# Two transformer-like layers over 16 batches: a new order of the stages on PE, ACT, DVE and GpSimd

## The chip, the core and the metric

The kernel runs on one core of one Trainium2 chip. The metric is the time of one execution on the device, in microseconds (us). Engines are named as the profile names them: PE is TensorE (its weight loads are PEld), DVE is VectorE, ACT is ScalarE, POOL is GpSimd, SP is SyncE, which issues only DMAs here. "The granted clock" is the share of its full speed that TensorE was granted in a stretch.

## What is computed

Sixteen batches of 548 tokens (36 of an image, 512 of text, 64 numbers each) pass through two layers. Each line adds its result to `h`:

```
h = concat(patches @ W + b, table[x_txt] + positions)
h = h + attention(layernorm(h))          # relu attention, FFN 64->128->64, layernorm
h = h + experts_top1(layernorm(h))       # argmax expert of 8, 1370 slots each, relu MLP 64->256->64
h = h + linear_attention(layernorm(h))   # per-head k and v normalised, kv = k^T v, q kv, proj, gelu
h = h + experts_top2(layernorm(h))       # 8 experts of 64->256->64 with gelu, weights of the best two
```

Only the second expert layer is computed densely: all eight experts see every token, and the two chosen ones are weighted. The first one moves tokens: each token's normalised row is scattered to its expert's slots in DRAM, the slots are computed, and each token gathers its row back.

## The kernel before, in words

The work is written as small stages, one function each, for a batch or a unit. `t1`, `q`, `k`, `scores0` to `scores4`, `attend_a` to `attend_c`, `ffn1`, `gate`, `count` are PE's in layer one; `norm1a`, `q_low`, `resid`, `norm3a`, `place` are DVE's there. `place` finds each token's slot; POOL's `scatter_a` and `scatter_b` then write the rows, five indirect DMAs a batch (L1079). Between the layers stands stage B: 32 units of the first expert layer, each turned (`b_turn`, L1322), multiplied (`b_up`, L1140 and L1141), multiplied back (`b_down`, L1340) and turned back (`b_back`, L1347). POOL gathers the rows of each batch (L497).

Layer two runs, for each batch: `mixed` on DVE (L430 to L442, L758 and L760: the gathered rows are weighted, limited and added to `H`), `mixed_stats`, `norm4` (L778 to L781), `t4` and `kv` on PE (L1111, L1118), `kv_b` (L788), `square` on ACT (L683), `sum_squares` (L794), `roots_kv` (ACT L664), `kvnorm_inv` and `kvnorm` (L799 to L808), `gram` (PE L563), `gram_s` (L816), small products, `pre_bias` (L847), `gelu_proj` (ACT L689), `norm5`, `t5`, `route` (L602) with its DVE stages, and then the dense experts: 18 tiles of 8 units, each unit `up` (PE L1140 and L1141), `gelu` (ACT L715), `down` (PE L628, two units at a time), `weigh` (DVE L978), `summed` (POOL L538); `back` and `finish` (DVE L990) close a tile. The dense experts of one batch run beside the linear attention of later ones.

Some stages stand once: `moe_bias` on PE (L1307), `moe_gains` (L1586, L1589) and `low_moe` (L1595) on DVE, `high_w` (L1466) and `high_moe` (L1470) on ACT prepare the weights of the experts. `fill` is three matmuls of ones (L1147) whose result nobody reads; 44 of them stand at numbered places.

What sets the order on each engine is a table, not the code. Each stage has a time in a period of 32 (for batch b, 32 b is added), each (stage, number) may have an entry in `..._MOVED` that is added to it, and `in_order` sorts:

```
plan.append((when + b * PERIOD + moved.get((name, b), 0), len(plan), name, b))
...
return [(name, b) for _, _, name, b in sorted(plan)]
```

Each engine runs its list strictly in order; its stages wait on semaphores that count the stages of other engines. A bank of PSUM is taken by `banks.take`, which makes the stage wait for the reader of the stage that took the bank before it in this order. ACT has three sets of functions in use (Sqrt, Gelu, Exp; Identity and Relu are in all), and where its list goes from a function of one set to one of another, an ACT_TABLE_LOAD stands in between.

Of the kernel before, what the change touches and what calls it, by code (L numbers as in the profile page):

```python
# [60 lines left out]
           mixed=12, weighted=5, norm4=3, kvnorm=3, fold=3, resid2=11, norm5=4, route_a=11, route_b=6)  # L61
# [73 lines left out]
def early_fusion_kernel(nc, i, out):  # L135
    with ExitStack() as ctx:
# [106 lines left out]
        def at(s):  # L243
# [11 lines left out]
        POOL_ONE = ((8.25, "gather_a"), (18.5, "gather_b"), (134.75, "offset"), (384, "scatter_a"), (396.75, "scatter_b"))  # L255
        PE_ONE = ((93.75, "t1"), (106.5, "q"), (115, "k"), (130, "scores0"), (132.5, "v"), (136, "scores1"), (140.25, "scores2"),
                  (145.25, "attend_a"), (150.75, "scores3"), (153.5, "attend_b"), (155.5, "scores4"), (162.5, "attend_c"), (170.25, "o_turn"),
                  (185.25, "t2"), (189.5, "ffn1"), (203.5, "ffn2"), (217, "y_turn"), (273, "t3"), (273.25, "gate"), (286.5, "count"))
        ACT_ONE = ((47.25, "roots1"), (98.5, "stack1"), (108.25, "q_high"), (123, "k_high"), (137, "relu0"), (139, "relu1"), (144.5, "relu2"),
                   (154.25, "relu3"), (159.5, "relu4"), (168, "o_copy"), (189.25, "stack2"), (198.5, "ffn_relu"), (207, "y_copy"), (226.5, "root2"),  # L260
                   (253.75, "root3"), (275.5, "stack3"))
        DVE_ONE = ((25.25, "norm1a"), (41.75, "norm1b"), (104, "q_low"), (112.25, "k_low"), (127.25, "vals"), (168.75, "resid"), (212.25, "norm2a"),
                   (226.25, "norm2b"), (237.25, "norm3a"), (254.75, "norm3b"), (268.5, "gate"), (285.75, "place"))
# [114 lines left out]
        gram_s, kv_g, kv_s, a_s, fold_b = ff[0][0:D + 1, 0:D + 1], ff[0][0:D, 128:128 + D], ff[0][0:D, 256:256 + D], ff[0][0:D, 384:384 + D + 1], ff[1][:, 0:D]  # L378
# [1493 lines left out]
```

## Time and profile before

| | |
|---|---|
| median of 3 runs | 848.64 us (847.61 to 850.04) |
| span of the profiled execution, first to last instruction | 846.4 us |
| PE busy | 729.7 us, 86% of the span |
| DVE busy | 612.2 us, 72% |
| ACT busy | 481.7 us, 57% |
| POOL busy | 433.1 us, 51% |
| mean granted clock of TensorE | 0.935 |

The profiled execution has no other time of its own than its span. The median of the runs is 2.2 us above it, which is what lies around the first and last instruction; a time that is worked out within the span is to be read with these 2.2 us added. In the run of time, layer one takes 0 to 287 us, stage B 298 to 372 us, the start of layer two 372 to 474 us, and from there the tiles of the dense experts end every 25 us or so until the last two (images) close the span.

### The profile page before, as it was taken

Reading aid. Unit: us, or ns where it says so; the run is one execution under the profiler, and the core shown is the slowest. Engines: PE = TensorE matmul, PEld = TensorE weight load, DVE = VectorE, ACT = ScalarE, POOL = GpSimd, SP = SyncE. Lnnn points to the kernel's source line nnn. Section 1 sums busy time; section 2 is a strip of 40 time slices with the busy share of each in tenths; the row PEclk is TensorE's granted clock in tenths of the full one; section 3 lists DMA queues with packets and bytes.
Section 4 is the critical chain, followed back from the end, with each engine's and each line's share of the span. In section 5 each row is a group of like instructions: output and inputs, shape, how many; then the busy total and the mean of one; then the engine's idle time right before and its main releaser. Section 6 shows DMA issues by size and latency. Waiting matters only on the chain.

```text
span 846.4 us, 15831 instructions
## 1 busy us (share of the span) xinstructions
PE 729.7 (86%) x4619; PEld 487.1 (58%) x4619; DVE 612.2 (72%) x2308; ACT 481.7 (57%) x980; POOL 433.1 (51%) x470
## 2 busy tenths in 40 slices
PE   3589999999988689965789989989989999899995
PEld 1366777666655257643456555556555656566672
DVE  4557899989678536576777889888888977786231
ACT  1255655555541146642246877766788666777552
POOL 5732617773764600246646667667676763223222
PEclk8599999999997889995679999999999999999988
DMA  7910000000000023220022221222221122223200
GB/s 216 359 53 9 14 8 19 22 21 5 5 4 3 4 58 97 75 66 12 6 57 57 62 56 17 57 59 63 62 63 41 31 55 61 62 62 61 62 14 7
DMA packets 60976, 43.69 MB, mean 52 GB/s; under 512 B 29100, under 2 KB 56252, under 8 KB 60636
## 3 DMA queue, kind: packets, MB, share of 16 engines
q1 hardware_dynamic: 51820, 36.35, 17.2%
q0 software_dynamic: 7200, 4.17, 2.4%
q10 hardware_dynamic: 1872, 2.18, 0.9%
q8 instruction: 38, 0.62, 0.3%
q14 instruction: 46, 0.38, 0.1%
HBM read 31.66 MB, written 13.47 MB: 53 GB/s over the span
## 4 chain that ended last, share of the span: by engine, by line
PE 26%; ACT 15%; DVE 14%; issue 9%; POOL 2%; DMA 1%; DVEq 0%; ACTq 0%; POOLq 0%
ACT scratch L715 7%; PE psum L628 6%; PE psum L1140 5%; PE psum L1141 4%; ACT L715 3%; PE psum L1340 3%; ACT L664 2%; PE psum L1147 2%; DVE xt L788 1%; PE psum L1322 1%; PE psum L1118 1%; PE psum L602 1%; ACT L659 1%; DVE kh L885 1%; DVE stats L1507 1%
## 5 line engine op out<-in xcount | busy, mean ns | idle before, releaser
L715 ACT ACTIVATE scratch<-psum,fb 128x512 f32<-128x512 f32 (+2 forms) x288 | 172.2, 665 | 37.4 <-PE psum L1141 36.1
L628 PE MATMUL psum<-scratch,w_fw 128*64 128x256 f32 (+2 forms) x1152 | 141.7, 383 | 11.4 <-DVE scratch L978 5.7
L538 POOL TENSOR_TENSOR prob<-prob,scratch 128x256 f32<-128x256 f32 (+2 forms) x126 | 79.3, 629 | 141.0 <-DVE scratch L978 139.4
L497 POOL DMA_INDIRECT uu<-expert_out,slot_i x80 | 83.2, 1040 | 88.3 <-issue 68.7
L1079 POOL DMA_INDIRECT slots_buf<-xt,slot_i x80 | 82.5, 1032 | 68.0 <-DVE slot_i L1754 45.8
L628 PEld LDWEIGHTS psum<-scratch,w_fw 128*64 128x64 f32 x1152 | 79.1, 140 | 56.5 <-DVE scratch L978 13.5
L1065 POOL DMA_INDIRECT emb<-in_table,w_ids x64 | 63.4, 991 | 55.8 <-DVE stats L1507 33.5
L1405 ACT ACTIVATE prob<-psum 128x292 f32<-128x292 f32 (+1 forms) x160 | 55.1, 396 | 52.2 <-PE psum L1207 52.1
L1140 PE MATMUL psum<-kh,fw_hi 128*128 128x512 f32 x176 | 80.0, 455 | 0.6 <-ACT scratch L715 0.5
L1141 PE MATMUL psum<-kh,fw_lo 128*128 128x512 f32 x176 | 71.8, 408 | 0.0
L978 DVE SCALAR_TENSOR_TENSOR scratch<-psum,w_fb,X 128x256 f32<-128x256 f32 (+1 forms) x119 | 54.4, 460 | 16.9 <-PE psum L628 15.5
L1206 PE MATMUL psum<-qst,kh 128*128 128x292 f32 (+1 forms) x160 | 53.8, 350 | 2.4 <-DVE kl L1635 1.2
L1216 PE MATMUL psum<-prob,vv 128*64 128x256 f32 (+1 forms) x320 | 49.8, 410 | 1.3 <-ACT prob L1405 1.3
L683 ACT ACTIVATE xt<-xt 128x640 f32<-128x640 f32 x16 | 11.8, 737 | 63.8 <-DVE xt L788 63.8
L1507 DVE BATCH_NORM_STATS2 stats<-H 128x6 f32<-128x64 f32 x320 | 46.6, 213 | 1.5 <-issue 0.4
L1140 PEld LDWEIGHTS psum<-kh,fw_hi 128*128 128x128 f32 x176 | 34.5, 196 | 19.3 <-ACT scratch L715 6.8
L1140 PE MATMUL psum<-kl,fw_hi 128*128 128x512 f32 (+2 forms) x112 | 45.4, 411 | 0.0
L1766 DVE TENSOR_TENSOR qst<-psum,qst 64x256 fp32r<-64x256 f32 (+2 forms) x32 | 16.5, 518 | 37.8 <-ACT qst L1490 37.7
L1207 PE MATMUL psum<-qst,kl 128*128 128x292 f32 (+1 forms) x160 | 43.4, 292 | 0.0
L1147 PE MATMUL psum<-ones_b 128*128 128x512 bf16 x132 | 38.8, 436 | 3.3 <-ACT scratch L715 2.0
L1141 PE MATMUL psum<-kl,fw_lo 128*128 128x512 f32 (+2 forms) x112 | 41.5, 378 | 0.0
L1206 PEld LDWEIGHTS psum<-qst,kh 128*128 128x128 f32 x160 | 30.7, 192 | 17.9 <-issue 12.9
(272 smaller groups left out, 1715.7 us busy)
## 6 DMA issues: line engine op xcount, KB each, us to landing
X<-share_buf SPq DMA_DIRECT2D x32, 512.0 KB
slots_buf<-zeros SPq DMA_DIRECT2D x8, 352.0 KB, 4.9
expert_out<-zeros SPq DMA_DIRECT2D x8, 352.0 KB, 4.9
out<-H SPq DMA_DIRECT2D x16, 128.0 KB
X<-in_patches ACTq DMA_DIRECT2D x3, 576.0 KB, 7.3
slots_buf<-xt,slot_i POOLq DMA_INDIRECT x80, 2.2
uu<-expert_out,slot_i POOLq DMA_INDIRECT x80, 2.5
emb<-in_table,w_ids POOLq DMA_INDIRECT x64
```

The costliest lines, as they stand in the source:

```text
L497: pool.indirect_dma_start(yg[b % 2][0:rows, s, :], None, expert_out, bass.IndirectOffsetOnAxis(slot_i[0:rows, b, (s + 1) % SLOTS:(s + 1) % ...
L538: pool.tensor_tensor(total[t % 2][:, 0:z], total[t % 2][:, 0:z], part[m % PARTS][:, 0:z], ALU.add).then_inc(sem("summed"), 1)
L628: last = pe.matmul(bank(6 + n % 2)[h * D:(h + 1) * D, 0:z], w["fw2"][:, e * J + j, :], hid[(J * n + j) % (J * UNITS)][:, h * z:(h + 1) * z ...
L715: act.activation(hid[m % (J * UNITS)][:, 0:z], bank(2 + m % 4)[:, 0:z], ACT.Gelu, bias=fb1[:, e * J + j:e * J + j + 1]).then_inc(sem("gelu ...
L1065: pool.indirect_dma_start(emb[b % 2][:, t, :], None, i["table"], bass.IndirectOffsetOnAxis(w["ids"][:, b * TXT + t:b * TXT + t + 1], 0)).t ...
L1079: pool.indirect_dma_start(slots_buf, bass.IndirectOffsetOnAxis(slot_i[0:rows, b, (s + 1) % SLOTS:(s + 1) % SLOTS + 1], 0), xt3[b % XT3][0: ...
L1140: pe.matmul(dst, parts[0][:, cols], rhs, start=True, stop=False)
L1141: return pe.matmul(dst, parts[1][:, cols], rhs, start=False, stop=True)
L1147: pe.matmul(bank(FILLED).rearrange("p (k n) -> p k n", k=4), ones_b[:], bs(ones_b[:], 4), start=True, stop=True)
L1206: pe.matmul(dst, kh[b % 2][:, at(s):at(s) + P], q_side, start=True, stop=False)
L1405: act.activation(prob[s][:, FIRST[h]:FIRST[h] + z], bank(SCORE[h])[:, 0:z], ACT.Relu, scale=SCALE).then_inc(sem("relu"), 1)
L1507: st(dve.bn_stats(stats[:, s, :], src[:, s, :]))
```

## The change: what it does

The tables POOL_ONE, PE_ONE, ACT_ONE, DVE_ONE (layer one), POOL_TWO, PE_TWO, ACT_TWO, DVE_TWO (layer two) and the four MOVED tables have other numbers; the MOVED tables grow from some 50 lines to some 400, with an entry for nearly every stage and batch. Nothing else in the file changes: the functions, the once-tables, the lists of fills and the lags of the experts' units are as they were. Line numbers of the new file are those of the old one plus 348 behind the tables (L1147 is now L1495, L1589 is L1937, L788 is L1136, L715 is L1063).

```diff
-        PE_ONE = ((93.75, "t1"), (106.5, "q"), (115, "k"), (130, "scores0"), (132.5, "v"), (136, "scores1"), (140.25, "scores2"),
+        PE_ONE = ((80.125, "t1"), (107.25, "q"), (119.125, "k"), (136.875, "scores0"), (119.875, "v"), (141.375, "scores1"), (145.75, "scores2"),
...
-        PE_TWO = ((74.25, "t4"), (78.75, "kv"), (94, "gram"), (97.5, "gains_k"), (101.5, "by_q"), (104.75, "by_proj"), (114.5, "proj"), (130, "t5"),
+        PE_TWO = ((74.125, "t4"), (83, "kv"), (101.375, "gram"), (105, "gains_k"), (108.5, "by_q"), (111.875, "by_proj"), (120.375, "proj"),
```

Of the MOVED tables, new entries are for instance `("moe_bias", 0): -599.839` on PE, `("moe_gains", 0): -559.402` and `("low_moe", 0): -571.34` on DVE, `("high_moe", 0): -659.064` on ACT: these stages go from the end of layer one to its start. `("fill", 16): -3.257` to `("fill", 35): -189.54` gather fills ahead of stage B, and `("up", 0): -26.809` brings the first unit of the dense experts forward.

Every engine has the same stages as before. The only instructions whose number differs are ACT's table loads: 60 before, 72 now.

**Place one, the end of layer one.** DVE before, at the last but one batch: statistics of `norm3a`, then `moe_gains` (L1586, L1589), then the gate (L1719 on).

```order
L1674 TENSOR_TENSOR zt<-zt,rs 128x320
L1676 TENSOR_TENSOR zt<-zt,w_fg 128x320
L1679 TENSOR_TENSOR H<-H,zt 128x320
L1507 BN_STATS stats<-H 128x6 x5
L1510 BN_AGGR mv_1<-stats 128x2 x5
L1586 TENSOR_TENSOR fb1<-psum,w_fb1 128x16
L1589 TENSOR_SCALAR scratch<-scratch,w_fln_g 128x256 x8
L1591 ISA
L1719 TENSOR_TENSOR g_lg<-psum,w_gb 128x40
```

DVE now, at the same place:

```order
L2022 TENSOR_TENSOR zt<-zt,rs 128x320
L2024 TENSOR_TENSOR zt<-zt,w_fg 128x320
L2027 TENSOR_TENSOR H<-H,zt 128x320
L1855 BN_STATS stats<-H 128x6 x5
L1858 BN_AGGR mv_1<-stats 128x2 x5
L2067 TENSOR_TENSOR g_lg<-psum,w_gb 128x40
L2069 TENSOR_REDUCE g_mx<-g_lg 128x5
```

`moe_gains` now stands behind `norm1a` of batch 4, near the start; `low_moe` (L1595), which stood between the last gate and the last `place`, stands behind `k_low` of batch 2.

PE before, from the last `count` (L1297, L1300) to the first `b_turn` (L1322) of stage B:

```order
L1147 MATMUL psum<-ones_b 128x512 x3
L1297 MATMUL psum<-oh_b,tri_b 128x40
...
L1300 MATMUL psum<-oh_b,ones_b 128x8
L1147 MATMUL psum<-ones_b 128x512 x30
L1322 MATMUL psum<-w_ident,X 64x128 x6
L1140 MATMUL psum<-qst,ew_hi 128x384
L1141 MATMUL psum<-qst,ew_lo 128x384
```

PE now, at the same place:

```order
L1495 MATMUL psum<-ones_b 128x512 x3
L1645 MATMUL psum<-oh_b,tri_b 128x40
...
L1648 MATMUL psum<-oh_b,ones_b 128x8
L1495 MATMUL psum<-ones_b 128x512 x69
L1670 MATMUL psum<-w_ident,X 64x128 x6
L1495 MATMUL psum<-ones_b 128x512 x3
L1488 MATMUL psum<-qst,ew_hi 128x384
L1489 MATMUL psum<-qst,ew_lo 128x384
```

There are 69 matmuls of ones ahead of the first `b_turn` where 30 stood, and no fills further on in stage B.

**Place two, the start of layer two.** PE before, from the last `b_back` (L1347): `t4` (L1111) and `kv` (L1118) of batch 0, then `gram` (L563) of batch 0, and `t4` of batch 1 only behind the small products.

```order
L1347 MATMUL psum<-w_ident,X 128x128 x2
L1147 MATMUL psum<-ones_b 128x512 x3
L1111 MATMUL psum<-w_ident,xt 128x128 x3
L1118 MATMUL psum<-w_wkv,ot 128x256 x2
L1118 MATMUL psum<-w_wkv,ot 36x128
L1147 MATMUL psum<-ones_b 128x512 x3
L563 MATMUL psum<-scratch 65x65 x5
L569 MATMUL psum<-ff,ak 64x65
```

PE now:

```order
L1459 MATMUL psum<-w_ident,xt 128x128 x3
L1695 MATMUL psum<-w_ident,X 128x128
L1495 MATMUL psum<-ones_b 128x512 x3
L1466 MATMUL psum<-w_wkv,ot 128x256 x2
L1466 MATMUL psum<-w_wkv,ot 36x128
L1495 MATMUL psum<-ones_b 128x512 x21
L1459 MATMUL psum<-w_ident,xt 128x128 x3
L1466 MATMUL psum<-w_wkv,ot 128x256 x2
L1466 MATMUL psum<-w_wkv,ot 36x128
L911 MATMUL psum<-scratch 65x65 x5
```

`t4` of batch 0 now stands ahead of the last `b_back`, and `t4` and `kv` of batch 1 ahead of `gram` of batch 0. The first `up` (L1140, now L1488) stood behind `route` and the small products of batches 1 and 2; now it stands right behind `route` of batch 0 (L950, L951). On DVE the same place reads, before (`norm4`, `mixed`, statistics, `kv_b`, `sum_squares`):

```order
L781 TENSOR_TENSOR xt<-zt,rs 128x320
L430 TENSOR_TENSOR uu<-uu,top_w 128x320
...
L760 TENSOR_TENSOR H<-H,prob 128x320
L1507 BN_STATS stats<-H 128x6 x5
L1510 BN_AGGR mv_1<-stats 128x2 x5
L788 TENSOR_TENSOR xt<-psum,w_kv_b 128x640
L794 TENSOR_REDUCE prob<-xt 128x160
L799 TENSOR_SCALAR prob<-prob 128x160
```

and now:

```order
L2130 COPY X<-psum 128x128 x2
L1136 TENSOR_TENSOR xt<-psum,w_kv_b 128x640
L778 TENSOR_TENSOR uu<-uu,top_w 128x320
...
L1108 TENSOR_TENSOR H<-H,prob 128x320
L1855 BN_STATS stats<-H 128x6 x5
L1858 BN_AGGR mv_1<-stats 128x2 x5
L1142 TENSOR_REDUCE prob<-xt 128x160
L1126 RECIPROCAL rs<-sd_1 128x5
L1127 TENSOR_TENSOR zt<-H,mv_1 128x320
```

`kv_b` of batch 0 (L788, now L1136) stood behind `mixed` of batch 1 and stands ahead of it; `norm4` of batch 1 (now L1126) stands right behind the statistics it needs.

**Place three, ACT in the tiles of the dense experts.** Before, one batch's worth: the loads go to Sqrt for `roots_kv` (L664), to Gelu (L715), to Sqrt for `roots4` (L659), to Gelu.

```order
L715 ACTIVATE scratch<-psum,fb 128x512 x2
L664 ACT_TABLE_LOAD
L664 ACTIVATE prob<-prob 128x160
L670 ACTIVATE sd_0<-mv_0,eps_t 128x5
L671 ACTIVATE sd_0<-mv_0,eps_t 128x5
L715 ACT_TABLE_LOAD
L715 ACTIVATE scratch<-psum,fb 128x512 x4
L725 ACTIVATE ff<-psum 40x128
L659 ACT_TABLE_LOAD
L659 ACTIVATE sd_0<-mv_0,eps_t 128x5
L715 ACT_TABLE_LOAD
L715 ACTIVATE scratch<-psum,fb 128x512 x2
```

Now, in one of the early tiles, `roots5` (L1018, L1019) no longer stands beside `roots_kv` (L1012), and has loads of its own:

```order
L1012 ACT_TABLE_LOAD
L1012 ACTIVATE prob<-prob 128x160
L1063 ACT_TABLE_LOAD
L1063 ACTIVATE scratch<-psum,fb 128x512 x2
L1037 ACTIVATE vv<-vv 128x320
L1063 ACTIVATE scratch<-psum,fb 128x512 x4
L1018 ACT_TABLE_LOAD
L1018 ACTIVATE sd_1<-mv_1,eps_t 128x5
L1019 ACTIVATE sd_1<-mv_1,eps_t 128x5
L1073 ACTIVATE ff<-psum 40x128
L1063 ACT_TABLE_LOAD
L1063 ACTIVATE scratch<-psum,fb 128x512 x2
```

Six loads stand in a batch's worth instead of four, in about six of the tiles; two fewer stand in a few late ones; the sum is the 12 more.

## Rows read from the trace of the kernel before

**Rows 1.** The page's head and part 1.
```profile
span 846.4 us, 15831 instructions
PE 729.7 (86%) x4619; PEld 487.1 (58%) x4619; DVE 612.2 (72%) x2308; ACT 481.7 (57%) x980; POOL 433.1 (51%) x470
```
**Rows 2.** Stretches: from:to, length, each engine's busy us (instructions), clock, DMA share, GB/s.
```profile
0.00:42.00 42.00, 19.35 (x86) 12.08 (x86) 20.38 (x102) 9.50 (x21) 26.98 (x32) 0.72 0.88 287
42.00:85.00 43.00, 39.15 (x241) 27.57 (x242) 29.70 (x117) 23.78 (x66) 14.60 (x16) 1.00 0.11 34
296.00:339.00 43.00, 39.84 (x291) 28.30 (x292) 20.46 (x58) 25.33 (x55) 0.00 (x0) 0.92 0.27 77
```
**Rows 3.** The same view, for layer two: its start, two periods, its end.
```profile
372.00:434.00 62.00, 36.78 (x156) 20.93 (x155) 44.94 (x161) 13.93 (x29) 35.73 (x35) 0.66 0.14 30
434.00:472.00 38.00, 34.65 (x207) 23.25 (x208) 29.55 (x121) 28.08 (x48) 22.58 (x25) 0.96 0.16 33
472.00:497.00 25.00, 22.52 (x146) 14.62 (x146) 21.49 (x77) 18.43 (x32) 17.53 (x20) 1.00 0.25 54
797.00:822.00 25.00, 25.00 (x198) 18.78 (x195) 7.17 (x18) 13.53 (x33) 6.18 (x14) 0.87 0.26 55
```
**Rows 4.** Timeline of DVE, end of layer one: start us, us, operation, idle before.
```profile
264.33 0.20 DVE L1719 TENSOR_TENSOR g_lg<-psum,w_gb 128x40 f32<-128x40 f32 x1 [1.27 <-PE psum L1130]
...
274.58 2.60 DVE L1589 TENSOR_SCALAR scratch<-scratch,w_fln_g 128x256 f32<-128x256 f32 x8
...
283.29 2.28 DVE L1595 TENSOR_TENSOR fw_lo<-scratch,fw_hi 128x2048 fp32r<-128x2048 f32 x1
```
**Rows 5.** Timeline of ACT and of POOL, end of layer one.
```profile
280.86 1.90 ACT L1470 ACTIVATE fw_hi<-scratch 128x2048 fp32r<-128x2048 f32 x1
...
281.94 0.99 POOL L1079 DMA_INDIRECT slots_buf<-xt,slot_i  x1 [3.92 <-DVE slot_i L1754]
...
294.34 0.91 POOL L1079 DMA_INDIRECT slots_buf<-xt,slot_i  x1 [0.30 <-issue]
```
**Rows 6.** Timeline of PE, end of layer one and start of stage B.
```profile
266.59 4.37 PE L1307 MATMUL psum<-w_fln_b,scratch 64*128 64x1 f32 x32
...
283.68 8.04 PE L1147 MATMUL psum<-ones_b 128*128 128x512 bf16 x30
298.51 1.46 PE L1322 MATMUL psum<-w_ident,X 128*64 128x128 f32 x6 [6.79 <-issue]
...
305.23 1.08 PE L1340 MATMUL psum<-scratch,w_ew 128*64 128x256 f32 x8
```
**Rows 7.** Timeline of DVE, start of layer two.
```profile
374.86 0.49 DVE L430 TENSOR_TENSOR uu<-uu,top_w 128x320 f32<-128x320 f32 x1 [1.68 <-DMA uu<-expert_out,slot_i]
...
379.08 0.79 DVE L788 TENSOR_TENSOR xt<-psum,w_kv_b 128x640 f32<-128x640 f32 x1
...
387.62 0.19 DVE L778 RECIPROCAL rs<-sd 128x5 f32<-128x5 f32 x1 [0.25 <-issue]
```
**Rows 8.** Timeline of PE, start of layer two.
```profile
384.42 1.52 PE L563 MATMUL psum<-scratch 128*65 128x65 f32 x10 [7.78 <-DVE scratch L808]
...
433.63 0.79 PE L1140 MATMUL psum<-kh,fw_hi 128*128 128x512 f32 x1
```
**Rows 9.** Timeline of DVE: `finish` of the first tile and of the second.
```profile
473.94 0.41 DVE L990 TENSOR_TENSOR H<-H,psum 128x256 f32<-128x256 f32 x1
...
498.81 0.41 DVE L990 TENSOR_TENSOR H<-H,psum 128x256 f32<-128x256 f32 x1
```
**Rows 10.** ACT by lines: the costliest group of table loads (busy, mean ns, idle before).
```profile
L715 ACT ACT_TABLE_LOAD x27 | 34.6, 1283 | 0.5
```
**Rows 11.** Timeline of ACT in a period of layer two.
```profile
568.02 1.27 ACT L715 ACTIVATE scratch<-psum,fb 128x512 f32<-128x512 f32 x2
569.31 1.28 ACT L664 ACT_TABLE_LOAD   x1
570.60 0.34 ACT L664 ACTIVATE prob<-prob 128x160 f32<-128x160 f32 x1
```

More of the change, by code:

```diff
@@ L259, in early_fusion_kernel @@
[L259 to L263, printed above, removed]
+        POOL_ONE = ((-45.875, "gather_a"), (-38.875, "gather_b"), (81.375, "offset"), (317.5, "scatter_a"), (345.375, "scatter_b"))
@@ L283, in early_fusion_kernel @@
-        PE_MOVED = {("attend_b", 0): -1.5, ("attend_b", 14): 2, ("attend_c", 0): -2, ("attend_c", 15): 1.5, ("back", 16): 1, ("back", 17): 14,
-                    ("by_q", 0): 3, ("by_q", 1): 0.75, ("by_q", 2): -0.25, ("by_q", 3): 0.75, ("count", 1): -3, ("count", 12): 1, ("down", 130): 4,
-                    ("down", 131): 4, ("down", 132): 3, ("down", 133): 3, ("down", 134): 3, ("down", 135): 3, ("down", 136): 8, ("down", 137): 8,
-                    ("down", 138): 8, ("down", 139): 8, ("down", 141): 8, ("down", 143): 8, ("ffn1", 1): -0.75, ("ffn1", 15): 3, ("ffn2", 13): -1.5,
-                    ("ffn2", 15): -1.25, ("gains_k", 0): 4.25, ("gains_k", 1): -0.5, ("gains_k", 15): 0.5, ("gains_k", 2): -0.75, ("gate", 15): -6,
-                    ("gram", 0): -8.5, ("gram", 1): 0.5, ("gram", 2): -0.75, ("gram", 3): 2.75, ("kv", 1): -2, ("kv", 3): 0.75, ("o_turn", 1): 5,
-                    ("o_turn", 14): -0.5, ("o_turn", 15): -2.5, ("o_turn", 2): 6, ("proj", 2): 0.75, ("proj", 3): 1.25, ("route", 1): -2.5,
[5 rows of a table removed]
@@ new lines, in early_fusion_kernel @@
+        DVE_TWO = ((33.558, "mixed"), (43.225, "mixed_stats"), (49.125, "norm4"), (85.375, "kv_b"), (90.375, "sum_squares"), (95.625, "kvnorm_inv"),
+                   (98.75, "kvnorm"), (103.75, "gram_s"), (106.25, "own_heads"), (109.75, "add_input"), (113.5, "fold"), (124.08, "pre_bias"),
+                   (126.375, "resid2"), (127.25, "resid2_stats"), (135.125, "norm5"), (140.5, "low5_even"), (141.125, "low5_odd"),
+                   (144.25, "route_logits"), (147.375, "route_first"), (151.25, "route_next"), (156.125, "route_second"), (159.125, "route_shares"))
```

345 lines of the change are left out of this document (301 added, 44 removed), and 130 rows, old and new, of tables (ACT_MOVED, DVE_MOVED, PE_MOVED).

## Prediction, made before the changed kernel ran

> **What bounds the kernel now.** I read the shares of the engines first, then the stretches, then the places where an engine stood idle. PE is busy 86% of the span, DVE 72%, ACT 57% and POOL 51% [rows 1], but these are averages over stages with different limits. In layer one PE hardly stops: 39.15 of 43 us from 42 us on at full clock [rows 2], so an order that only shuffles stages there has little to give. Only its first 42 us are loose: PE 19.35, DVE 20.38, ACT 9.50 us busy, with the DMA engines at 0.88 [rows 2]. Stage B is PE's too (39.84 of 43 us [rows 2], most of the rest before its first matmuls). Two places are not bound by any engine's work. At the start of stage B, PE ends its fills near 291.7 (283.68 and 8.04 us) and stands 6.79 us until the slots' rows come at 298.51 [rows 6]. In the start of layer two, 372 to 434 us, PE is busy 36.78 of 62 us, fills among it, and DVE 44.94, at a granted clock of 0.66 [rows 3]: there the chain of small stages of the first batches sets the pace, and the dense experts, which could fill PE, begin only at 433.63 [rows 8]. Then the tiles come at a period of 24.87 us (from 473.94 to 498.81 [rows 9]); per 25 us PE is busy 22.52, DVE 21.49, ACT 18.43 [rows 3]. No engine is full: the wait goes round between them. At the end PE is full again, 25.00 of 25 [rows 3].
>
> **The change part by part.**
>
> *The stages that stand once.* `moe_bias` (4.37 us of PE [rows 6]), `moe_gains` and `low_moe` (2.60 and 2.28 us of DVE [rows 4]) and `high_moe` (1.90 us of ACT [rows 5]) go from the end of layer one to its start. There they fall on engines that are less than half busy, so I cost them at nothing. If that cover is gone, because the weights land late under the 0.88 of DMA, PE stands in front of `moe_bias` and all batches shift; the bounds for this are 0 and 4.4 us, nearer 0. At the other end, DVE's row up to the last slots becomes shorter by 2.60 + 2.28 = 4.9 us, and the 1.27 us idle before the gate [rows 4] can be filled as well. But the slots are not the only thing the last scatters wait for. POOL issues ten scatters from 281.94 to 294.34 + 0.91 [rows 5], 1.28 us each, and needs these 13.3 us from the moment the first slots of batch 14 exist. Those come earlier by the 2.60 us of `moe_gains` and part of the 1.27, so the last scatter ends 2.8 to 3.5 us earlier. The rows of the first unit then lie ready near 295 to 295.7, in place of 298.5.
>
> *The fills ahead of stage B.* 69 matmuls stand where 30 stood. The 30 took 8.04 us [rows 6], 0.268 each; 69 take 18.5 us at that rate. The last `count`, right behind which the fills began at 283.68, follows the gate and comes 4.9 us earlier with it, near 278.7, so PE is free at 297.2 by this rate; the rate itself may be better if the clock is (I allow 2 us). So the fills reach about as far as the data, 295 to 297. This gains 1.4 to 3.5 us at the first `b_turn`, and because PE has not stood idle before, the first units do not run at the lower clock as they do before; with two fills no longer standing ahead of `b_down`, which begins at 305.23 only [rows 6], that is another 1 to 2.5 us. I take 3.5 us for this place together; bounds 0 (fills longer than the data) and 6.
>
> *Stage B itself.* The order of `b_turn`, `b_up`, `b_down`, `b_back` was a regular round of four and is irregular now (two `b_turn` in a row, two `b_back` in a row). PE was full there, so it can only lose: I take 1.5 us, bounds 0 and 3.
>
> *The start of layer two.* Before, `kv_b` of batch 0 at 379.08 stood behind `mixed` and the statistics of batch 1, which themselves waited 1.68 us for a gather from 374.86 [rows 7]. Now it stands ahead, and can run as soon as PE gives it: `t4` of batch 0 lies inside stage B now, and behind the last `b_back` (372) only a fill and `kv` are left, so near 373.6. The 4.2 us of `mixed` and statistics come behind it, so `sum_squares` of batch 0, and with it `gram` (384.42, after 7.78 us of idle PE [rows 8]), gains only about 1 us. The gain is in batch 1: its `norm4`, at 387.62 before [rows 7], follows its statistics at once, near 381; its `kv` is on PE before `gram` of batch 0. Batch 2 follows the same way, by my count of the stages between some 10 us earlier. The first `up`, at 433.63 [rows 8], stands right behind `route` of batch 0 and can begin near 407. That does not shorten the span by 26 us: in 372 to 472 us DVE has 44.94 + 29.55 = 74.5 us of work [rows 3], and what is left idle, 25 us in 100, is all that can be won. The expert units of tile 0 are now fed between the small stages. Summing DVE's stages in the new order up to the first `finish`, with the durations of before, gives about 461 in place of 473.94 [rows 9], but with 3.6 us of DVE's work for later batches not yet done. I take a lead of 10 us, bounds 5 and 14.
>
> *The steady periods.* PE's order hardly changes there; DVE's `mixed` and `norm4` come earlier, and the units are grouped unevenly. What costs is on ACT: 12 more table loads, nearly all in tiles of the first half. A load takes 1.283 us [rows 10], and nothing beside it: the ACTIVATE before ends at 569.29, the load begins at 569.31, the next ACTIVATE at 570.60 [rows 11]. Together 12 x 1.283 = 15.4 us of ACT. A tile with six loads has ACT at 18.43 + 2.6 = 21.0 of 24.9 us, still less than PE or DVE, so most of it is hidden. But `gelu` feeds `down` and `weigh`, and a load in front of it is a delay in the round that sets the period. I take a sixth of it less what the earlier `norm4` gives back: 2 us lost; bounds -12 (PE's idle 2.4 us a period, over 13 periods, won back by nearly half) and +12 (most loads on the path).
>
> The Trainium skill, "ScalarE: Activation LUTs", section "What ACT_TABLE_LOAD costs", counts a drain of about 1380 ns with each load of about 1283 ns, 2.66 us for a switch. The load agrees with the trace, the drain does not show in it, since the next instruction begins where the load ends; by the page's figure the 12 loads would be an estimated 32 us of ACT, and the forecast sum would turn into a loss if half of that were on the path. I go by the rows.
>
> *The end* is full of PE's work in nearly the same order, so a lead that is there at 797 us is kept.
>
> The sum: -3.5 +1.5 -10 +2 = -10 us, against the profiled span of 846.4: 836.4, and with the 2.2 us that the median lies above that span, 838.6 us.
>
> **The rivals.**
>
> *ACT's loads eat the lead (slower).* If each extra load falls into the round (the `gelu` of a unit waits, PE's `down` waits for it, DVE's `weigh` for that), 15.4 us [rows 10] are lost, more than the 12 won elsewhere: -3.5 +1.5 -10 +15.4 = +3.4, 852.0 us. The point from which it decides is a tile whose ACT has more than the period of 24.87 us in work and waits for `xt`; for it speaks that a load stands between two ACTIVATEs with no slack on either side [rows 11], against it ACT's 6.6 idle us of 25 [rows 3].
>
> *An uneven layer one loses (slower).* PE is busy 39.15 of 43 us there [rows 2] and each engine runs strictly in order, so a stage placed ahead of its data stops its engine. With 1 us for each of 13 batches, 848.6 - 10 + 13 = 851.6. For it speaks that single entries move a stage by whole periods; against it that stages of one batch lie many microseconds apart, with other batches between them.
>
> *The periods shrink too (faster).* If the new order takes half of PE's 2.4 idle us of each of 13 periods, 15.6 us more and no 2 us lost: 838.6 - 17.6 = 821.0. For it: neither PE nor DVE is full. Against: PE's own order is nearly the old one, and ACT has more to do.
>
> *The lead is given back (no change).* The early `up` units run ahead, and then wait in the first periods for `share` rows, DMAs on SP's queue, or a bank; finish of tile 5 comes where it did. Then only stage B's part is left, and 848.6 - 2 = 846.6 or more, up to 850.
>
> **How the numbers follow.** My forecast has 0.50, its own range 829 to 848. The loads 0.18, layer one 0.10, shrinking periods 0.12, the lead given back 0.10. A difference of less than 0.3%, 2.5 us, can't be told from no change. Faster: nearly all of the forecast (0.47), all of the shrinking periods (0.12) and a little of the others (0.04), 0.63. Slower: most of the two slower rivals, 0.25. The same: 0.12. The range reaches from 825 (half of the fast rival is left out) to 853 (a third of the slow ones is left out).
>
> **What would show it.** In the changed kernel's profile: the last scatter ends near 292; the first `b_turn` begins at 295 to 297, with less than 2 us idle before it and a clock near full; `kv_b` of batch 0 within 3 us of the last `b_back`; the first `up` near 407; the first `finish` near 458 (461 less the 3 us won before), so 15 or 16 us before its old place, a part of which is not real; and the sixth `finish` about 12 us before its old place. It is wrong if stage B begins later than 298.5, if PE's busy share in 42 to 254 us falls by more than 2 points, or if the period of tiles 1 to 4 is over 25.5 us; then the loads have got into the round.

## The result: 30 us less, three times what was forecast

The new order takes 819.15 us (median of 4 runs, 817.05 to 823.86) against 849.34 us of the kernel before (847.61 to 851.33): a ratio of 0.965, with a 95% interval of 0.9616 to 0.9685. Run again later, beside other kernels, it took 816.75 us, a ratio of 0.9621 (0.9592 to 0.9651). The forecast was 838.6 us with a range of 825 to 853; the measured time lies below it, next to the number of the rival that had the periods shrink (821.0 us, chance 0.12), which it meets in part by luck, as is worked out below.

The page of the new kernel, its head and part 1, against [rows 1]:

```profile
span 822.1 us, 15850 instructions
PE 731.4 (89%) x4619; PEld 500.8 (61%) x4619; DVE 631.0 (77%) x2308; ACT 499.2 (61%) x992; POOL 435.9 (53%) x470
```

The matmuls are the same 4619, PE's busy time is 1.7 us more, and the span is 24.3 us less: the change took away PE's idle time, 116.7 us before and 90.7 now. This profiled execution, with its span of 822.1 us, is the longest of its four runs. A second profile of the same kernel, from the later runs, has a span of 813.3 us and is the shortest of its six. Both begin stage B at the same time to 0.04 us, and they part in stage B and layer two (the first has a stretch of lower clock, 0.80 against 0.93 for 522 to 547 us), by up to 8.8 us at the end. So a number that comes from layer two is good here to about 4 us to either side, and where only one profile is used, the text says which.

The end of layer one and the start of stage B in the first profile of the new kernel, timeline of POOL and of PE, against [rows 5, 6]:

```profile
285.88 0.92 POOL L1427 DMA_INDIRECT slots_buf<-xt,slot_i  x1 [0.30 <-issue]
```
```profile
277.38 15.98 PE L1495 MATMUL psum<-ones_b 128*128 128x512 bf16 x69
293.20 0.82 PE L1670 MATMUL psum<-w_ident,X 128*64 128x128 f32 x6
...
297.29 1.08 PE L1688 MATMUL psum<-scratch,w_ew 128*64 128x256 f32 x8
```

The last scatter ends at 286.80 in place of 295.25: 8.5 us earlier, where I had forecast 2.8 to 3.5. The first `b_turn` follows at 293.20 and the first `b_down` at 297.29, 7.9 us earlier. The single stages stand at the start now (timelines of PE and of DVE; L1655 is `moe_bias`, L1483 the `k` behind it, L1943 `low_moe`), against [rows 4, 6]. `high_w` on ACT moves as well, from 91.67 to 36.15 us, which my prediction did not list:

```profile
26.35 6.98 PE L1655 MATMUL psum<-w_fln_b,scratch 64*128 64x1 f32 x32
33.27 2.20 PE L1483 MATMUL psum<-xs,w_wk 128*128 128x292 f32 x4
```
```profile
58.40 2.28 DVE L1943 TENSOR_TENSOR fw_lo<-scratch,fw_hi 128x2048 fp32r<-128x2048 f32 x1
```

The start of layer two in the first profile, timelines of DVE and of PE, against [rows 7, 8]. L1136 is `kv_b` of batch 0, L1126 `norm4` of batch 1, L911 `gram` of batch 0, L1488 the first `up`:

```profile
368.19 0.82 DVE L1136 TENSOR_TENSOR xt<-psum,w_kv_b 128x640 f32<-128x640 f32 x1 [1.60 <-PE psum L1466]
...
373.84 0.18 DVE L1126 RECIPROCAL rs<-sd 128x5 f32<-128x5 f32 x1
```
```profile
380.06 1.55 PE L911 MATMUL psum<-scratch 128*65 128x65 f32 x10 [0.92 <-DVE xt L1136]
...
400.32 0.79 PE L1488 MATMUL psum<-kh,fw_hi 128*128 128x512 f32 x1
```

Stretches of both kernels between the same events, the later profile of the new kernel below (its columns are those of [rows 2]). The events are the first `b_turn`, the last copy of stage B, `finish` of tile 0 and of tile 8, and the end (the two `finish` to 0.6 us):

```profile
42.00:298.50 256.50, 230.34 (x1484) 160.69 (x1485) 204.30 (x854) 127.62 (x341) 139.19 (x135) 0.97 0.06 15
298.50:371.90 73.40, 71.58 (x533) 49.67 (x534) 42.01 (x120) 46.51 (x98) 9.67 (x10) 0.97 0.27 78
371.90:473.90 102.00, 73.43 (x374) 45.40 (x372) 76.46 (x283) 43.90 (x79) 60.04 (x60) 0.78 0.15 31
473.90:672.90 199.00, 180.56 (x1136) 116.92 (x1135) 171.03 (x608) 145.70 (x249) 138.96 (x152) 0.99 0.25 53
672.90:846.40 173.50, 154.46 (x1011) 102.32 (x1009) 98.00 (x344) 108.48 (x195) 58.20 (x83) 0.95 0.23 48
```
```profile
0.00:42.00 42.00, 26.31 (x124) 20.42 (x125) 23.28 (x118) 11.54 (x25) 24.61 (x29) 0.76 0.89 286
42.00:293.20 251.20, 229.49 (x1478) 164.02 (x1477) 210.32 (x838) 127.45 (x337) 138.92 (x138) 0.97 0.07 16
293.20:364.90 71.70, 70.16 (x529) 48.28 (x528) 44.33 (x124) 44.97 (x99) 10.90 (x11) 1.00 0.27 78
364.90:451.30 86.40, 67.57 (x336) 43.16 (x336) 72.52 (x260) 45.18 (x77) 60.36 (x60) 0.76 0.16 35
451.30:647.30 196.00, 180.96 (x1154) 119.40 (x1149) 179.75 (x641) 156.94 (x258) 154.28 (x164) 0.99 0.25 54
647.30:813.30 166.00, 150.37 (x1009) 102.13 (x1007) 98.36 (x331) 112.92 (x199) 45.50 (x70) 0.95 0.23 50
```

Length less PE's busy time is PE's idle time. Before and now: 22.6 and 15.7 in the first 42 us, 26.2 and 21.7 in the rest of layer one, 1.8 and 1.5 in stage B, 28.6 and 18.8 in the start of layer two, 18.4 and 15.0 in tiles 1 to 8, 19.0 and 15.6 behind them. Idle time fell in every part of the program but stage B, where the first profile has 2.9. I had seen a part of the first and the fourth, and had put down the tiles as a small loss.

These numbers count the matmuls of ones, which nobody reads, as work. They take PE 21.3 us before and 27.6 now (later profile) in layer one, 3.3 and 1.3 in stage B, and 14.2 and 5.3 in the start of layer two. So more than half of the 11.4 us that went from PE's idle time in layer one was filled with them, and idle time and fills together fell there by 5.2 us only. In the start of layer two they fell by 18.7, while 3 us more of real work stand in a stretch that is 15.6 us shorter.

The lead of `finish`, the time by which it comes earlier (`finish` of 474, 499, 648, 673, 700 and 837 us of before; the first and the fourth row below answer to [rows 9]):

| | tile 0 | tile 1 | tile 7 | tile 8 | tile 9 | tile 15 |
|---|---|---|---|---|---|---|
| new kernel, first profile | 19.1 | 13.9 | 13.9 | 18.3 | 25.4 | 24.3 |
| new kernel, later profile | 22.5 | 17.3 | 21.1 | 25.6 | 32.6 | 33.1 |

As forecast, tile 0's lead is partly not real, and 5 us of it are gone at tile 1. Then the first profile has no net change up to tile 7 and the later one 3.8 us more, and in both 11.5 us are won in tiles 8 and 9.

### The profile page after: what moved, and what is told of

It is laid out like the page before. It is cut to its first block and busy times, and to the rows that moved or that the text cites. A ratio compares the mean times of both kernels' runs of the same rounds, so it can differ in the third digit from the quotient of the medians.

```text
span 822.1 us, 15850 instructions
## 1 busy us (share of the span) xinstructions
PE 731.4 (89%) x4619; PEld 500.8 (61%) x4619; DVE 631.0 (77%) x2308; ACT 499.2 (61%) x992; POOL 435.9 (53%) x470
## 5 line engine op out<-in xcount | busy, mean ns | idle before, releaser
L1063 ACT ACTIVATE scratch<-psum,fb 128x512 f32<-128x512 f32 (+2 forms) x288 | 172.9, 667 | 54.5 <-PE psum L1489 45.8
L976 PE MATMUL psum<-scratch,w_fw 128*64 128x256 f32 (+2 forms) x1152 | 144.9, 393 | 5.9 <-DVE prob L1326 4.1
L886 POOL TENSOR_TENSOR prob<-prob,scratch 128x256 f32<-128x256 f32 (+2 forms) x126 | 82.2, 652 | 107.8 <-DVE scratch L1326 102.3
L1427 POOL DMA_INDIRECT slots_buf<-xt,slot_i x80 | 80.4, 1004 | 67.1 <-DVE slot_i L2102 45.5
L976 PEld LDWEIGHTS psum<-scratch,w_fw 128*64 128x64 f32 x1152 | 83.6, 144 | 47.8 <-issue 16.3
L1488 PE MATMUL psum<-kh,fw_hi 128*128 128x512 f32 x176 | 80.2, 456 | 1.9 <-ACT scratch L1063 1.9
L1326 DVE SCALAR_TENSOR_TENSOR scratch<-psum,w_fb,X 128x256 f32<-128x256 f32 (+1 forms) x119 | 53.6, 464 | 25.6 <-PE psum L976 24.8
L1753 ACT ACTIVATE prob<-psum 128x292 f32<-128x292 f32 (+1 forms) x160 | 55.0, 398 | 25.8 <-PE psum L1555 24.4
L1488 PE MATMUL psum<-kl,fw_hi 128*128 128x512 f32 (+2 forms) x112 | 47.5, 428 | 1.5 <-ACT scratch L1063 1.5
L1564 PE MATMUL psum<-prob,vv 128*64 128x256 f32 (+1 forms) x320 | 47.4, 405 | 0.0
L1847 ACT ACTIVATE scratch<-psum,w_eb 128x256 f32<-128x256 f32 (+2 forms) x64 | 32.0, 550 | 24.7 <-PE psum L1489 24.3
L1488 PEld LDWEIGHTS psum<-kh,fw_hi 128*128 128x128 f32 x176 | 34.7, 197 | 18.5 <-ACT scratch L1063 6.9
L1063 ACT ACT_TABLE_LOAD x32 | 41.1, 1283 | 4.5 <-PE psum L976 4.0
L1489 PE MATMUL psum<-kl,fw_lo 128*128 128x512 f32 (+2 forms) x112 | 43.2, 389 | 0.0
L875 POOL TENSOR_TENSOR ex<-euler,mx 128x5 f32<-128x5 f32 x16 | 19.4, 1212 | 38.6 <-DVE lg L1281 38.2
L1554 PEld LDWEIGHTS psum<-qst,kh 128*128 128x128 f32 x160 | 30.7, 192 | 12.2 <-issue 5.5
```

Source lines behind the costliest of these rows:

```text
L886: pool.tensor_tensor(total[t % 2][:, 0:z], total[t % 2][:, 0:z], part[m % PARTS][:, 0:z], ALU.add).then_inc(sem("summed"), 1)
L976: last = pe.matmul(bank(6 + n % 2)[h * D:(h + 1) * D, 0:z], w["fw2"][:, e * J + j, :], hid[(J * n + j) % (J * UNITS)][:, h * z:(h + 1) * z ...
L1063: act.activation(hid[m % (J * UNITS)][:, 0:z], bank(2 + m % 4)[:, 0:z], ACT.Gelu, bias=fb1[:, e * J + j:e * J + j + 1]).then_inc(sem("gelu ...
L1326: dve.scalar_tensor_tensor(out=dst[:, 0:z], in0=bank(6 + n % 2)[:, 0:z], scalar=w["fb2"][:, e:e + 1], in1=tile_share(t, e)[:, 0:z], op0=AL ...
L1427: pool.indirect_dma_start(slots_buf, bass.IndirectOffsetOnAxis(slot_i[0:rows, b, (s + 1) % SLOTS:(s + 1) % SLOTS + 1], 0), xt3[b % XT3][0: ...
L1488: pe.matmul(dst, parts[0][:, cols], rhs, start=True, stop=False)
```

## The experiments

In the first six, whole pieces of the order were taken from one kernel or the other. The old tables stand beside the new ones, and on each engine layer two follows one order for its first stages (the number in CUT) and the other for the rest:

```diff
+def in_order(engine, layer, new, old, others=()):
+    if layer == "ONE":
+        return by_times(*(new if ONE_IS == "new" else old), others)
+    first, rest = (by_times(*(new if which == "new" else old), others) for which in (FIRST_IS, REST_IS))
+    ahead = first[:CUT[engine]]
+    return ahead + [stage for stage in rest if stage not in ahead]
```

All ratios are to the kernel before in the same job.

**Layer one new, the rest old** (`ONE_IS = 'new'; FIRST_IS, REST_IS = 'old', 'old'`).

> Layer one in the new order, stage B and layer two in the old one. Theory A (the gain is a sum over places): the lead that the new kernel has when its first b_down begins, 7.9 us (297.29 against 305.23), is made by layer one and by the fills ahead of stage B; only the first is here, so slot_i of the last batches comes near 279 in place of 287, stage B begins 5 to 8 us earlier and all of it is kept: the kernel before less 5 to 8 us. Rival B (the lead is made by the fills alone, layer one is worth what the moved single stages are worth): less 3 us or nothing.

838.82 us against 849.54, a ratio of 0.987 (0.984 to 0.9899): 10.7 us less. The lead is 10.3 us at the last slots, 8.6 through stage B and 7.2 to the end. Theory A holds, and layer one is worth more than either theory gave it. This kernel has 39 matmuls of ones ahead of the first `b_turn`, nine more than before, but they end while the rows are still on their way: PE stands 5.36 us behind them, and `b_turn` begins 3.3 us after the last scatter, as before. So its lead owes nothing to the fills.

**Layer one old, the rest new** (`'old'; 'new', 'new'`).

> Layer one in the old order, stage B and layer two in the new one. Theory A: what is left of the 24 to 30 us when layer one's 6 to 8 us are taken off, so the kernel before less 17 to 22 us. Rival B: less 22 to 27 us. If the two parts do not add up (e1 and e2 together more than 4 us from the whole), the places are not independent.

827.03 us, 0.9738 (0.9713 to 0.9763): 22.5 us less. The two parts together give 33.2, the whole 30.2: they add up within what is measured. A part of the 3.0 us can be named: here 60 matmuls of ones end just as the rows come, and the time from the last scatter to the first `b_down` is 7.4 us, where it is 10.0 before and 10.5 in the new kernel, whose 69 run beyond the data.

**Stage B and the start of layer two new** (`'old'; 'new', 'old'`, CUT PE 231, DVE 215, ACT 125, POOL 60).

> Layer one old; stage B and the first stages of layer two, up to about the first finish, in the new order; all that comes later in the old order. Theory A: the lead of finish of tile 1 and later (14 us in the new kernel, 5 to 6 of them from layer one) is made here and kept to the end, so less 8 to 11 us. Rival C (a lead made early is given back unless the later order uses it): less 0 to 4 us.

837.52 us, 0.9856 (0.9829 to 0.9884): 12.0 us less. `finish` of tile 1 leads by 9.3, of tile 8 by 9.1 and of tile 15 by 10.0: a lead is kept, and is not given back. Timeline of PE in this kernel, the fills and the first `b_turn`:

```profile
282.97 14.47 PE L1584 MATMUL psum<-ones_b 128*128 128x512 bf16 x60
297.75 1.01 PE L1759 MATMUL psum<-w_ident,X 128*64 128x128 f32 x6 [0.31 <-issue]
```

From the last scatter (294.52) to the first `b_down` (301.83) it takes 7.3 us in place of 10.0. The first `b_down` leads by 3.4 us, the last copy of stage B (370.54) by 1.4, and the rest is won in the start of layer two. My forecast had 8.5 us for stage B and the start of layer two (-10 +1.5). That part was right.

**Only the end of layer two new** (`'old'; 'old', 'new'`, CUT PE 351, DVE 381, ACT 214, POOL 141).

> Layer one, stage B and layer two up to about its middle (batch 10, tile 6) in the old order, the rest in the new one. Theory A: tiles 9 to 11 of the new kernel take 12 us less than before, the last ones give 6 back, so less 6 to 12 us. Rival C (the late order gains only because it comes with a lead and with the stages that stand ahead of it): within 3 us of the kernel before, or slower.

855.69 us, 1.0075 (1.0048 to 1.0102): 6.2 us more. But the trace shows two things: `finish` of tile 7 is 20.2 us late, and that of tile 11 only 2.9. The seam, where stages of batches 11 and 12 that the new order wants later and the old one had not done meet, costs 17 us (between 620 and 670 us ACT waits 7.3 us in one piece for a batch's statistics, and PE 7.5 us for a `gelu`), and the new order wins them back in four tiles. In the last four it loses 6.8 us again, as the new kernel does in its first profile (31.1 us of lead at tile 11, 24.3 at tile 15), so some of what tiles 8 to 11 win is work put off. Neither theory had the seam.

**New up to about tile 7** (CUT PE 369, DVE 407, ACT 228, POOL 158).

> Layer one old; stage B and layer two in the new order until about tile 7's middle, the rest old. With the new order up to the first finish only, the kernel took 12.0 us less than before; with all of layer two new 22.5 less. If the late tiles (8 to 11, 25 us each before, 20 to 21 in the new order) make the difference: 12 to 14 less than before. If the middle tiles have already prepared it (stages of later batches done ahead): 18 to 22 less.

834.27 us against 850.86, 0.9802 (0.9753 to 0.9851): 16.6 us less, between the two expectations, with an interval that meets that of the start alone. In the trace, `finish` of tile 8 leads by 8.3 and of tile 15 by 10.5, no more than with the start alone, but the profiled run is the slowest of the four (837.79 us). So whether the tiles up to 7 give nothing or some 4 us stays open.

**New up to about tile 9** (CUT PE 440, DVE 497, ACT 279, POOL 191).

> Layer one old; layer two new until about finish of tile 9, the rest old. With the new order to the first finish 12.0 us less than before, to tile 7 16.6 less, throughout 22.5 less. If the gain is made in tiles 8 and 9 (periods of about 20 us in the new order against 25 before): 19 to 23 less. If only the last tiles (10 to 17) make it: 12 to 17 less.

827.69 us against 849.74, 0.9741 (0.9702 to 0.978): 22.0 us less, all that the new layer two gives. Its `finish` leads by 14.7 at tile 7, 19.2 at tile 8, 26.2 at tile 9, and then by 19 to the end. The 10 us that come on top of the start are made in the tiles up to 9. The 11.5 us of tiles 8 and 9 come alike in all four profiles that have the new order there, but here 7 of them go again in tiles 10 and 11, where the old order sets in. The share of the tiles up to 7 can't be told from profiles: with the same order up to there, `finish` of tile 7 leads by 6.5, 7.4 and 14.7 us in three kernels. The last tiles add nothing.

**Single stages moved alone, in the kernel before.**

```diff
+        PE_MOVED = {("moe_bias", 0): -580.5, ...
+        DVE_MOVED = {("moe_gains", 0): -587.75, ("low_moe", 0): -586.2, ...
+        ACT_MOVED = {("high_w", 0): -145.1, ("high_moe", 0): -663, ...
```

> The kernel before with only the single stages moved from the end of layer one to its start: moe_bias, moe_gains, low_moe, high_w, high_moe. My prediction priced this at 2.8 to 3.5 us at the last scatter, against nothing at the start; stage B then begins about 3 us earlier: less 2.5 to 3.5 us. Rival: PE or DVE wait for the weights at the start (the DMA engines are busy 0.88 there) and the batches shift: less 0 to 1 us, or slower.

859.12 us against 849.39, 1.0116 (1.0052 to 1.018): 9.7 us more. Here `moe_bias` stands behind `v` of batch 0. Timelines of DVE and ACT in this kernel:

```profile
45.47 0.17 DVE L1586 TENSOR_TENSOR fb<-psum,w_fb 128x16 f32<-128x16 f32 x1 [6.42 <-PE psum L1307]
```
```profile
46.26 0.81 ACT L1405 ACTIVATE prob<-psum 128x292 f32<-128x292 f32 x2 [8.49 <-PE psum L1207]
```

DVE stood 6.42 us for `moe_bias`, and ACT 8.49 us for the scores behind it. `k` of the seventh batch and of all later ones comes 14.6 to 14.8 us later. At the end of layer one 4.7 us of that are won back (10.1 us at the last slots), near the 4.9 that I had counted, and 3.6 at the last scatter (306.41 for 295.25), for which I had 2.8 to 3.5. So the end of the move was priced right, and the start, which I had at nothing, was wrong for this place.

**The same with `moe_bias` ahead of `k` of batch 0** (`("moe_bias", 0): -598.6`), in the place where PE stood idle 4.97 us.

> The kernel before with the single stages moved to the start, but moe_bias ahead of k of batch 0, where PE stood idle 4.97 us, in place of behind v of batch 0. If what cost 14.8 us at the start in the first try was mostly PE's 4.4 us falling behind work: the batches shift by 7 to 11 us, and the kernel takes 2 to 6 us more than before. If DVE's and ACT's parts (moe_gains, low_moe, high_w, high_moe ahead of q_low and k_low) cost it: as in the first try, 8 to 10 us more.

852.99 us against 849.74, 1.0039 (1.0018 to 1.006): 3.3 us more. Timeline of PE in this kernel:

```profile
26.82 6.99 PE L1307 MATMUL psum<-w_fln_b,scratch 64*128 64x1 f32 x32
```

In the gap it takes 6.99 us, in place of 4.37 at the end of layer one [rows 6], and costs 2.3 us at `vals` of batch 0. The later batches shift by 9.0 us. The rest of the price, some 6 us, I put down to the stages on DVE and ACT; no run moves them alone. At the last slots 3.0 us are left. So even in its gap the move does not pay in the old layer one. In the new one it stands at the same place (26.35, until 33.27), and the last slots come earlier all the same.

**39 more matmuls of ones**, with the single stages moved as in the first try (`FILLS_B = (*[-23.5] * 13, ...)`).

> The same and 39 more matmuls of ones ahead of the first b_turn (69 in all, as in the new kernel). If the clock and not the data holds the first units of stage B: 1.5 to 3 us less than the kernel with the single stages moved alone, with the first b_down near 299 to 301. Rival: the fills last longer than the rows take to come, and it is the same or slower than without them.

856.68 us, 1.0082 (1.0054 to 1.011): 2.4 us less than without them, which their intervals do not tell apart. The traces give a cleaner measure, the time from the end of the last scatter to the first `b_down`: 10.0 us before (295.25 to 305.23), 10.0 with the single stages moved (306.41 to 316.43), 9.1 with the fills (304.53 to 313.67), and 10.5 in the new kernel (286.80 to 297.29).

**Fewer fills in the new kernel**, 54 matmuls in place of 69.

```diff
+        LEFT_OUT = range(20, 25)
-            return [(when, "fill", first + k) for k, when in enumerate(sorted(times))]
+            return [(when, "fill", first + k) for k, when in enumerate(sorted(times)) if first + k not in LEFT_OUT]
```

> The new kernel with 54 matmuls of ones ahead of the first b_turn in place of 69 (five fills left out). In the new kernel the last scatter ends at 286.8 and PE is busy with fills until 293.2, while before the rows came 3.3 us behind the last scatter. So the data is there near 290, and stage B begins 3 us earlier: 3 us less than the new kernel. Rival: the rows come only near 293 and nothing changes.

814.43 us, 0.9583 (0.9521 to 0.9644). Timeline of PE:

```profile
277.40 12.44 PE L1496 MATMUL psum<-ones_b 128*128 128x512 bf16 x54
289.88 0.49 PE L1671 MATMUL psum<-w_ident,X 128*64 128x128 f32 x3
...
290.68 0.52 PE L1671 MATMUL psum<-w_ident,X 128*64 128x128 f32 x3 [0.31 <-DMA X<-slots_buf]
...
293.96 1.08 PE L1689 MATMUL psum<-scratch,w_ew 128*64 128x256 f32 x8
```

PE leaves the fills as the rows arrive: it waits 0.31 us for the second of them. The time from the last scatter to the first `b_down` is 7.3 us (286.66 to 293.96), 3.2 less than in the new kernel. The fills of the new kernel were too long by just these. What 69 of them gave against 30 was nothing with this layer one; 60 gave 2.6 us with the old one, where the rows come later. Both kernels were run again on one chip.

> The new kernel once more, beside the one with fewer fills on the same chip: 0.960 to 0.970 of the kernel before.

> The new kernel with 54 in place of 69 matmuls of ones ahead of stage B, again, beside the new kernel itself: 3 to 5 us less than it, since the first b_turn began 3.3 us earlier (289.88 against 293.20) and the lead was kept to the end. If it is less than 1 us, the first run's 4.7 us were the measurement's.

816.75 us, 0.9621 (0.9592 to 0.9651), for the new kernel and 814.5 us, 0.9581 (0.9551 to 0.9611), with fewer fills: 2.3 us less, where the first traces give 3.3 at the first `b_turn` and the second pair 4.6 (288.62 against 293.24, of which 1.4 are an earlier last scatter). The intervals overlap, but both are ratios to the same runs of before. Six runs against six, the means are 817.2 and 814.2 us, 2.9 apart, with a 95% interval of some 0.7 to 5.2: that it beats the new kernel is shown, by how much is not. In the second trace the 54 fills end 1.2 us before the rows come. It beats the kernel before by 35 us.

**Twelve more table loads in the kernel before, by a moved stage.**

```diff
+        ACT_MOVED = {**{("roots5", b): 4 for b in range(4, 10)}, ...
```

> The kernel before with roots5 of batches 4 to 9 moved behind one more pair of units, so that it needs table loads of its own: 12 more loads, 72 in all, as the new kernel has. If all of them were on the path: 15.4 us more. My prediction took about a sixth of it, 2 to 3 us more. If the period is held by something else and a load is hidden: within 1.5 us of the kernel before.

862.28 us, 1.0182 (1.0105 to 1.026): 12.9 us more. `finish` goes from 1.6 us early at tile 1 to 15.0 late at tile 10, 16.6 us for 12 loads. What PE waits for in this kernel (525 to 663 us: us in total, times, longest), and the same row of before (524 to 648 us):

```profile
PE psum L569 <- DVE ff L816: 11.4, 5, 2.4
```
```profile
PE psum L569 <- DVE ff L816: 2.0, 5, 0.4
```

The wait is for `gram_s`, which stands behind `norm5` on DVE, and that waits 8.9 us in five times for the moved `roots5`, where no such wait shows before. So this run does not tell a load's price from that of a late stage.

**Twelve more loads and nothing moved**, in the kernel before and in the new one.

```diff
             def gelu(n):
+                if n in (13, 21, 29, 35, 43, 53):
+                    act.activation(roots_spare[:, n // POS:n // POS + 1], eps_t[:, 0:1], ACT.Sqrt)
```

> The kernel before with a Sqrt of one column, which nobody reads, ahead of six units' gelu (units 13, 21, 29, 35, 43, 53): 12 more loads and 6 tiny ACTIVATEs, no stage moved. If the load itself was the price in the run with roots5 moved (16.6 us): 15 to 17 us more. If that price came from roots5 being late, with DVE's norm5 and gram_s waiting behind it: 0 to 6 us more.

> The new kernel with the same six Sqrts ahead of the same units: 84 loads. If the new order hides a load: 0 to 4 us more than the new kernel, and less than what the same edit costs the old order. If loads are on the path in both: 12 to 17 us more.

Old order: 867.58 us against 850.86, 1.0224 (1.0171 to 1.0277), 16.7 us more, or 1.39 a load. New order: 829.2 us, 0.9767 (0.972 to 0.9813), which is 0.0117 above the new kernel's first ratio and 0.0146 above its later one, so 10 to 12 us, or 0.8 to 1.0 a load. Both prices are good to 4 or 5 us. I had let five sixths of a load be hidden. In the old order nearly nothing of it is. That the new order hides up to a third is likely and not shown. What PE waits for with the added loads in 455 to 700 us, in the new order, and in the same stretch of the new kernel's first profile:

```profile
PE psum L1490 <- ACT scratch L1063: 15.1, 9, 3.1
```
```profile
PE psum L1488 <- ACT scratch L1063: 3.4, 6, 1.3
```

`up` waits for `gelu` to free its bank, 11.7 us more.

**Eight loads fewer in the new kernel**, by `roots4` of four batches moved beside other stages of its set.

```diff
+        ACT_MOVED.update({('roots4', 4): -2.353, ('roots4', 5): 1.978, ('roots4', 6): -9.24, ('roots4', 8): -5.069})
```

> The new kernel with four of ACT's stages moved beside another that uses the same set: roots4 of batch 4 behind roots5 of batch 1, of 5 behind roots_kv of 4, of 6 behind roots5 of 3, of 8 behind roots5 of 5. 64 table loads in place of 72. If a load costs 1.38 us here as it did in the old order (16.6 us for 12): 11 us less than the new kernel. If ACT waits for PE anyway in these tiles (it waits 16.6 us for up there), or the moved roots4 now waits for its statistics or delays what stands behind it: no gain, or up to 8 us slower.

840.73 us, 0.9907 (0.9874 to 0.9939): some 21 us more than the new kernel by the ratios, with fewer loads. `finish` of tile 0 is 3.2 us late against the first profile, tile 1 12.0, tile 4 14.6, and it stays there: all is lost where the first stages moved stand. Timeline of ACT, `roots4` of batch 6, and what ACT waited for in 400 to 520 us, here and in the new kernel:

```profile
470.60 0.30 ACT L1008 ACTIVATE sd<-mv,eps_t 128x5 f32<-128x5 f32 x1 [6.37 <-DVE mv L1859]
```
```profile
ACT sd L1008 <- DVE mv L1859: 15.8, 3, 6.4
```
```profile
ACT sd L1007 <- DVE mv L1858: 4.3, 1, 4.3
```

Moved ahead of its statistics, it stops ACT for 6.37 us with the `gelu` of all units behind it, more than the two loads (2.6 us) that it saves.

## Why the prediction was wrong, and where it was right

*The single stages and the end of layer one.* The step that failed first is "I cost them at nothing", with the scatters 2.8 to 3.5 us earlier. In the old layer one the start costs 9.0 to 14.8 us at the middle batches and 3.3 to 9.7 us in all. Engines busy for less than half of 42 us are not cover: what counts is which stage is next behind the inserted one. The end gave about the 4.9 us counted (4.7 and 6.0 measured at the last slots). But the new layer one as a whole has its last slots 7.7 to 10.7 us earlier, in the seven profiles of kernels that share it. So its other moves must absorb the start's price and win 3 to 6 us beyond the 4.9; I had them at 0. PE's idle time in layer one fell by 11.4 us (22.6 + 26.2 to 15.7 + 21.7), against 6 us more of busy time, and the fills alone are 6.2 us more. Which of the moved stages does it, no run here tells.

*The fills.* I forecast PE in the fills to 295 to 297 with the data at 295; PE left them at 293.20. The rate was better than I took, 15.98 us for 69, but the data was there near 290. The step was mis-sized because it rested on the last scatter. The term in sum, -3.5 us, measured -7.9 at the first `b_down`, and its split was wrong: -8.5 from layer one and +0.5 from the fills. The reasoning behind the fills' own part holds where they end with the data: with 60 of them and the old layer one the way from the last scatter to the first `b_down` shrank by 2.6 us, and the first six `b_turn` matmuls took 1.01 us in place of 1.46. Not two fills but one left the way to `b_down`: one still stands at 293.86.

*Stage B.* Taken at 1.5 us lost. In the first profile the lead falls from 7.9 to 5.6 (371.91 against 366.30), 2.3 us; in the later one from 7.9 to 7.1. In the third run it falls from 3.4 to 1.4. Right, as far as it can be told.

*The start of layer two.* Taken at 10 us. Alone, with stage B, it gave 12.0 us of the time and 9 to 10 in the trace. `kv_b` of batch 0 came 1.9 us behind the last copy of stage B, `norm4` of batch 1 at 373.84 for 387.62, with `gram` 4.4 us earlier (I had said 1) and the first `up` at 400.32, 33 us earlier. From the last copy of stage B to tile 1 the lead grows by 8 to 10 us in these profiles. This step was right.

*The steady periods* are the step that failed most, and it was wrong twice. The forecast was 2 us lost, "a sixth" of 15.4 us for 12 loads less a little. The loads have most of their full price, 16.7 us in the old order and 10 to 12 in the new one; and yet layer two beyond its start gained 10.5 us (22.5 less 12.0). So the rest of the new order is worth some 20 us, if the loads it has cost what added ones do. I had set this at nothing because PE's order there "hardly changes". The new order reaches it in the tiles up to 9; with the late part alone the seam ate it. The fast rival had the right place and direction, but not its mechanism to size. It took half of PE's idle 2.4 us from each of 13 periods, 15.6 us. PE's idle time from `finish` of tile 0 to the end fell by 6.8 us (37.5 to 30.7 in the later profile, 30.1 in the first), less than a fifth. The other 3.7 us of that stretch's 10.5 in the later profile are less busy time, of which the first profile shows nothing. That the rival's 821.0 us lie so near the measured 819.15 is luck: its periods were too good by some 5 us, and the lead at stage B, which it shared with the forecast, was too small by 4.4.

*The rivals.* "ACT's loads eat the lead" was right on the price and wrong on the outcome. It needed that nothing else be gained in these tiles. "An uneven layer one loses" and "the lead is given back" are refuted by the first and third runs. The table load itself takes the same 1283 ns in both kernels (here the group behind L715's new number, by lines of ACT, against [rows 10]):

```profile
L1063 ACT ACT_TABLE_LOAD x32 | 41.1, 1283 | 4.5 <-PE psum L976 4.0
```

Its price, 1.39 us each in the old order, half a small ACTIVATE included, fits the rows, in which the next instruction begins where the load ends. The 2.66 us that the Trainium skill has for a switch ("ScalarE: Activation LUTs", section "What ACT_TABLE_LOAD costs") would be about 32 us for twelve, an estimate that both runs refute.

None of the signs of being wrong that I had named came: stage B began before 298.5 us, PE's busy share in 42 to 254 us fell by 1.6 points, and the period of tiles 1 to 4 was 25.4 us in the first profile and 24.4 in the later one. All three look for a loss, and the forecast failed by missing a gain.

*What stays open:* which moves in layer one and in tiles 2 to 9 win. The runs show the places and not the single moves, and no run mixes the order of one engine with the old orders of the others.

## What to carry to other kernels

In a kernel whose engines are tied in a round, 74% of busy time is not cover: an engine with 6.6 idle us of 25 passed on 1.39 us for each added load of 1.28. Price such an insertion at its full length, unless the profile shows that nobody waits behind it. Conversely, do not put a reordering at zero because one engine's own sequence looks alike: count the idle time of the engine that is busiest, stretch by stretch, as what can be won (116.7 us here, of which 28.3 went in the later profile), and give the case in which a tenth to a third of it goes more than a small chance. Count filler work with the idle time, or a wait that was only filled looks like a gain: together they were 155.5 us here and are 122.5 now. Size filler work by the arrival of the data, seen in a trace of the new order: 60 matmuls ended with the data in the old layer one, and 69 ran 3 us beyond it in the new one, where 54 ended with it.

## What the runs showed that I had not expected

A lead that is made early is kept almost whole: 7.2 of 8.6 us from stage B to the end with layer one alone, and with the start of layer two alone it stays between 8.6 and 11.3 us at every `finish` from tile 1 to tile 15, over 340 us. `moe_bias`, 32 matmuls of one column, takes 6.99 us at 27 us into the program, at a granted clock of 0.50, and 4.37 at 267 us, at 0.83. And a stage that was moved two units earlier to save two table loads of 1.28 us each stopped its engine for 6.37 us.
